# The layout of the transposed embedding rows: feature by feature instead of sample by sample

## The reference

```python
e = jnp.stack([tbl_0[ids[:, 0]], ..., tbl_26[ids[:, 26]]], axis=1)     # (512, 27, 128)
dot_products = jnp.einsum('bnd,bmd->bnm', e, e)                          # the "gram", one 27 x 27 per sample
r, c = np.tril_indices(27, k=-1)
z = dot_products[:, c, r]
h = jnp.concatenate([z, dense_ctx], axis=1)
h = jnp.maximum(h @ W_top1 + b_top1, 0.0)
h = jnp.maximum(h @ W_top2 + b_top2, 0.0)
y = h @ W_top3
```

## Time and profile before

| | |
|---|---|
| three runs | 153.29, 154.19, 155.78 us |
| the profiled execution | 153.77 us, span 152.0 us |
| PE busy, matmuls / weight loads | 106.0 us / 91.7 us |
| DVE busy | 65.1 us |
| ACT busy | 69.8 us |
| POOL busy | 69.1 us |
| mean granted clock of TensorE | 0.84 |

### The profile page before, as it was taken

One profiled execution on the slowest core, in us unless ns is written; L12 is line 12 of the kernel. 1 busy time (PEld: TensorE's weight loads), 2 busy tenths in 40 slices (PEclk: granted clock), 3 DMA queues, 4 the chain that ended last, 5 costly groups with the idle time before them and its releaser, 6 DMA issues.

```text
span 152.0 us, 3526 instructions
## 1 busy us (share of the span) xinstructions
PE 106.0 (70%) x1530; PEld 91.7 (60%) x1530; DVE 65.1 (43%) x96; ACT 69.8 (46%) x116; POOL 69.1 (45%) x74
## 2 busy tenths in 40 slices
PE   5987999993994190101143279999949949996694
PEld 5854778872893180000022169998849749896592
DVE  6699999997546300000063003898103212200500
ACT  3369999999280350000070007693406404660342
POOL 4778788787777777777057705407000000000000
PEclk9999999999689558555555556999999996999999
DMA  3976776796635551211002100201000000000000
GB/s 87 245 182 178 201 229 182 182 299 192 189 109 165 138 138 52 54 52 52 17 17 52 52 22 17 56 0 35 17 9 0 4 4 4 0 4 4 0 4 1
DMA packets 5433, 12.33 MB, mean 81 GB/s; under 512 B 1829, under 2 KB 2341, under 8 KB 5418
## 3 DMA queue, kind: packets, MB, share of 16 engines
q1 hardware_dynamic: 3306, 7.78, 18.3%
q0 software_dynamic: 2112, 4.33, 11.1%
HBM read 12.10 MB, written 0.00 MB: 80 GB/s over the span
## 4 chain that ended last, share of the span: by engine, by line
PE 41%; issue 31%; ACT 15%; DVE 7%; DMA 3%; SPq 2%; ACTq 0%
PE gram_ps L460 10%; PE ring L433 10%; PE ring L489 9%; ACT away L612 5%; PE ring L504 5%; DVE marks L553 4%; PE ring L444 4%; DMA raw<-tbl 3%; ACT high L598 3%; ACT marks L624 2%; DVE low L538 2%; ACT rowsT L657 2%; ACT rowsT L647 1%; PE ring L514 1%; SPq L322 1%
## 5 line engine op out<-in xcount | busy, mean ns | idle before, releaser
L360 POOL DMA_INDIRECT rows<-tbl,ids_sb x66 | 68.2, 1034 | 36.1 <-issue 18.9
L553 DVE TENSOR_TENSOR marks<-ids_ps,row_no 125x768 fp32r<-125x768 f32 (+1 forms) x38 | 39.7, 1077 | 36.6 <-remote 29.8
L460 PE MATMUL gram_ps<-rowsT 128*27 128x27 f32 x1024 | 16.1, 201 | 31.2 <-issue 31.2
L433 PE MATMUL ring<-marks,high 125*128 125x384 f32 (+1 forms) x92 | 36.5, 396 | 0.8 <-DVE low L538 0.5
L433 PE MATMUL ring<-marks,low 125*128 125x384 f32 (+1 forms) x92 | 35.3, 384 | 0.0
L460 PEld LDWEIGHTS gram_ps<-rowsT 128*27 128x27 f32 x1024 | 13.1, 112 | 34.6 <-issue 34.4
L433 PEld LDWEIGHTS ring<-marks,high 125*128 125x128 f32 x92 | 19.0, 206 | 4.2 <-DVE low L538 1.4
L433 PEld LDWEIGHTS ring<-marks,low 125*128 125x128 f32 x92 | 19.0, 206 | 1.4
L657 ACT COPY rowsT<-ring 128x512 f32<-128x512 f32 (+2 forms) x15 | 8.1, 555 | 21.5 <-remote 20.5
L647 ACT COPY rowsT<-ring 128x384 f32<-128x384 f32 (+1 forms) x11 | 11.1, 1009 | 14.0 <-remote 6.6
L538 DVE TENSOR_TENSOR low<-raw,high 125x512 fp32r<-125x512 f32 (+1 forms) x24 | 16.9, 705 | 0.0
(11 more groups left out here) (39 smaller groups left out, 76.2 us busy)
## 6 DMA issues: line engine op xcount, KB each, us to landing
raw<-tbl SPq DMA_DIRECT2D x9, 448.0 KB
raw<-tbl SPq DMA_DIRECT2D x2, 560.0 KB
rows<-tbl,ids_sb POOLq DMA_INDIRECT x66
w_sb<-w SPq DMA_DIRECT2D x2, 256.0 KB
w_sb<-w SPq DMA_DIRECT2D x1, 512.0 KB
raw<-tbl SPq DMA_DIRECT2D x9, 52.0 KB
raw<-tbl SPq DMA_DIRECT2D x2, 224.0 KB
w_sb<-w SPq DMA_DIRECT2D x1, 192.0 KB
```

The costliest lines, as they stand in the source:

```text
L360: nc.gpsimd.indirect_dma_start(out=rows[0:n, i % ROW_BUFS, s, :], out_offset=None, in_=tables[PLACES[s]], in_offset=bass.IndirectOffsetOnA ...
L433: last = nc.tensor.matmul(bank[:, 0:n], part[:, i % SPLIT_BUFS, c * D:(c + 1) * D], mark_of(unit, c), start=c == 0 and part is high, stop= ...
L460: last = nc.tensor.matmul(gram_ps[s * STRIP:s * STRIP + F, g, 0:F], places, places, start=True, stop=True)
L553: nc.vector.tensor_tensor(marks_of(unit), index.to_broadcast([TP, c1 - c0, n]), which.to_broadcast([TP, c1 - c0, n]), ALU.is_equal).then_i ...
```

## The change

`rowsT` becomes `[P, F, B]`: 27 features, and for each of them the 512 samples side by side. The padding goes. The features of one sample are now 512 floats, 2048 bytes, apart. The copy behind a find job writes one unbroken run of 512 or 384 floats. The copy behind a turn writes up to four runs of 128 floats and reads PSUM in its own order. The gram's two operands are the same 27 floats on each partition as before, read at a step of 2048 bytes, where they were side by side. Nothing else changes: no step, wait, engine, or count of instructions, and each engine keeps its order.

```diff
-F_PITCH = -(-F // PER_BANK) * PER_BANK
...
-        rowsT = sb("rowsT", [P, B, F_PITCH])
-        rowsT_f = rowsT[:, :, :].rearrange("p b f -> p f b")
+        rowsT = sb("rowsT", [P, F, B])
...
-                            places = rowsT[:, b0 + s * STRIP + g, 0:F]
+                            places = rowsT[:, 0:F, b0 + s * STRIP + g]
                             last = nc.tensor.matmul(gram_ps[s * STRIP:s * STRIP + F, g, 0:F], places, places,
                                                     start=True, stop=True)
...
-                    nc.scalar.copy(rowsT_f[:, place_of(i), b0:b0 + n],
+                    nc.scalar.copy(rowsT[:, place_of(i), b0:b0 + n],
                                    ring_bank(step)[:, 0:n]).then_inc(taken, 1)
...
-                    nc.scalar.copy(rowsT[:, b0:b0 + n, group[0]:group[-1] + 1],
-                                   src.rearrange("p (f b) -> p b f", b=n)).then_inc(taken, 1)
+                    nc.scalar.copy(rowsT[:, group[0]:group[-1] + 1, b0:b0 + n],
+                                   src.rearrange("p (f b) -> p f b", b=n)).then_inc(taken, 1)
```

## The result

The changed kernel took 158.8 us in the median of four runs (157.99 to 160.86); the kernel before, with one run more, 154.64 us. The ratio is 1.028, with a 95% interval of 1.017 to 1.039. In a later set of runs it was 1.046 (1.034 to 1.057). So it is slower in both sets, though the first interval doesn't settle whether by more than 2%; 158.8 us lies near the forecast of 157.5 and inside its range of 152.5 to 171. Some runs of each set were disturbed and took longer: the medians hold them, the ratios leave them out, so a ratio need not be the quotient of two medians, and for pad2052, held_before and held_again too few undisturbed runs were left to give one. The profiled execution took 158.86 us, its span is 157.0 us, 5.0 more than before.

A forecast was written before the change was run, and what follows sets the result against it. DVE and ACT are full from 8 to 38 us, gram 0 stalls from 47 to 77, PE is full outside the grams from 91; 153.77 + 3.5 + 0.2 - 0 = 157.5 us, range 152.5 to 171.

The forecast's parts named there:

- I took 0 with 1.1 as the end: ACT's shorter find copies, 5.8 us in all: 0 gained on the path, -1.1 us as the other end.
- no loss: Turn copies on ACT: neither gain nor loss, already 0.84 ns a float and now reading PSUM in order.
- +1.17 us: Bursts of each of grams 1 to 3: 3.69 us where 2.52, together 3.5 us.
- ACT's 1.97 ns a float: ACT's cost of single floats 112 bytes apart, taken for PE's gram columns: 28.8 ns a matmul.
- the pauses I keep as they are: Pauses inside grams 1 to 3: unchanged, though a slower burst could hide a few tenths of each.
- all of it reaches the end: Grams 1 to 3 have a full PE behind them, so their whole 3.5 us lengthens the kernel.
- I gave its burst 0.2 us: Gram 0's last 87 matmuls at half clock add 2.5 ns each, 0.2 us.
- Reads that hide it: Rival for the grams: PE fetches ahead, bursts stay at 2.5 us, 153.8 or 152.7 us; chance 0.24.
- A strip in series: Rival for the grams: a strip's loads and passes don't overlap, 53 ns a matmul, 169 us; chance 0.10.
- A shared path at 106 ns a matmul: Rival for the grams: four strips share one read path, 13.6 us a gram, 194 us; chance 0.08.
- the crawl: Gram 0's single records with idle time from 57 us; a shorter crawl had chance 0.10, a longer one 0.08.
- Loads and passes: In the grams, loads run beside passes and four strips beside each other: 24.3 ns estimated at half clock, 26.3 seen.

The follow-up runs named there:

- pad2052: The changed kernel with one float of padding behind each feature (step of 2052 bytes), second chip: 119.27 us against 119.35 for the kernel before, no ratio.
- held_before: The kernel before, with POOL's gathers of tile 2 held until gram 0 is done, second chip: 119.09 us against 119.35, no ratio.
- held_again: The kernel before, with POOL's gathers of tile 2 held until gram 0 is done, first chip: 149.26 us against 153.53, no ratio.
- copies_only: The changed kernel with both gram operands 27 floats side by side (what is computed is changed): 153.41 us against 153.51 for the kernel before, ratio 0.9964.
- pad2064: The changed kernel with four floats of padding behind each feature (step of 2064 bytes): 153.1 us against 153.51 for the kernel before, ratio 0.9953.
- step112: The kernel before, its gram reading one feature of 27 samples 112 bytes apart (what is computed is changed): 153.4 us, ratio 1.0033.
- second pair: The kernel before and the changed kernel, traced once more on the first chip: the span grows by 3.1 us, from 152.2 to 155.3.
- after_again: The changed kernel once more, against the kernel before on the first chip: 159.51 us, ratio 1.046 (1.034 to 1.057).

## Why the prediction was right

The forecast's direction and nearly its size were right, but much of that is luck: the mechanism that it priced costs this kernel nothing, and one that it hadn't foreseen, the collision of two 2048-byte steps, made it slower.

**Copies.** Right in size (0.58 and 0.49 us for the find copies) and in place: DVE and the empty stretch cover them, and copies_only shows a gain of less than 1.2 us where I took 0 with 1.1 as the end. What I had wrong is "no loss" for turn copies: they don't get longer by their own pattern (0.59 us), but the one beside gram 1 does, to 3.83 us. It ends inside the gram, and from gram 1 to gram 2 it takes 6.43 us where it took 6.41, so it cost nothing.

**Gram time.** The direction was right and two sizes were off, in opposite ways. I had +1.17 us for the bursts of each warm gram: 3.69 us forecast, 6.4 measured, +3.9. The step that failed is the one that took PE's cost from ACT's 1.97 ns a float at 112 bytes and ran loads and passes beside each other, both of them estimates; for steps other than 2048 it is a fair estimate (28.8 ns forecast, 32 measured in pad2064 and step112), and for 2048 on both operands it is not. The other step was "the pauses I keep as they are". They went: 1.99, 1.98 and 1.35 us. Net a gram costs +1.9, +1.9 and +2.5 us, where I had 1.17.

Pad2064 is the case that my working describes: far floats, with bursts of 4.0 to 4.14 us, somewhat longer than my 3.69. By my sum, in which all of that reaches the end, it would be over 4 us slower. It is not slower at all (ratio 0.9953), since shorter pauses and the clock behind gram 2 give the time back. So the step "all of it reaches the end" failed too, and without the collision of two 2048-byte steps the forecast of a slower kernel would have been wrong.

**Gram 0.** I gave its burst 0.2 us because at half clock, by my estimate, the array wants a column only every 1.80 ns. Its burst grew by 2.1 us and its end came 2.4 us later (0.9 in the second pair of traces), since a matmul takes 51 ns there, at half clock, as it takes 50 at full clock.

**Given back.** The 86 records between grams 2 and 3 take 10.0 us at full clock where they took 11.7 at 0.85, and a pause of 1.06 us after gram 3 is gone. I had no term for this. In the kernel before, the windows behind gram 2 and the layer's records there read:

```profile
124.70:128.20 3.50, 3.50 (x17) 3.50 (x18) 1.58 (x4) 1.37 (x4) 0.00 (x0) 0.51 0.02 5
128.20:136.40 8.20, 8.20 (x71) 7.53 (x69) 0.78 (x3) 5.03 (x12) 0.00 (x0) 1.00 0.00 0
...
124.58 4.57 PE L489 MATMUL ring<-zT,w_sb 128*128 128x128 f32 x24
```

The clock is at half for 3.5 us, just behind the pause of 1.98 us in gram 2; in the changed kernel, without the pause, it stays at 1.00, and the same 24 records take 3.02 us. The same holds in the second pair (4.58 and 3.00 us). That there is a pause doesn't decide it alone, since pad2064 has one of 1.53 us there and its clock stays at 1.00 as well. The sum of my terms, 3.7 us, is near the 5.0 measured because larger errors cancel: +10 us in the bursts (gram 0's among them), -5.3 in the pauses, -3.9 in the clock and the stretches between.

**Rivals.** Reads that hide it: PE doesn't hide them, since every pair of far operands takes 32 ns or more; but the rival's outcome, no slower kernel, is what every far step tried except 2048 on both operands gave. A strip in series: its 53 ns is near the 50 measured, but its mechanism isn't what the runs show, since pad2064 has the same reads in the same order at 32, and its 169 us is 10 us too long. A shared path at 106 ns a matmul falls. That the change would hardly move the crawl was right: gram 0's last burst begins at 88.99 us where it began at 88.66.

**Loads and passes.** That they run beside each other was my estimate, from the 26.3 ns of a matmul at half clock. The traces agree as far as one can see for dense reads and for far ones off 2048 bytes: dense, a matmul takes 19.7 ns where loads and passes in turn would take 4 x 27 x 0.90 / 4 = 24.3 (an estimate, from the 0.90 ns a column in the prediction), and both operands 112, 2052 or 2064 bytes apart (32 ns) cost no more than one at 2048 (34 and 35). With both at 2048 bytes a matmul takes 50 ns, and there the estimate doesn't hold. Why a far float costs PE more than a dense one, no run shows.

**Open.** Why 2048 bytes collide (pad2064 shows that it is the step; other large powers of two weren't tried), what makes the clock fall behind a dense gram 2 and not behind a slower one, what stalls the first chip, and how large the loss is: 2.8 and 4.6% in the two sets. The changed kernel itself wasn't run on the second chip. There gathers run beside grams 1 and 2, and may slow the dense ones too, so its cost there can't be read from these runs.

## What to carry to other kernels

When both operands of an f32 matmul are read float by float at a fixed step, don't let both steps be 2048 bytes: a padding of four floats here gives back what the layout cost (ratio 0.9953, a gram of 4.14 us for 6.41), and one float brings the gram down as far (4.16 us, on the second chip). A burst that got longer beside a pause for which the profile names nobody wasn't charged in full here (pad2064's three grams: 4.6 us more in the bursts, 1.4 to 1.9 in all); cost the pair, and look at the clock behind it (4.57 or 3.00 us for the same 24 records). Where a stall of 30 us has no cause that the trace shows, run the kernel on a second chip before building a version around it. And when a forecast comes out right, run the case that it described: here pad2064 showed that the case costs nothing.

## What the runs showed of the hardware

- Far floats on both operands make a gram's bursts about 1.6 us longer (32 against 19.7 ns a matmul), the same at 112, 2052 and 2064 bytes. ACT's find copies that write floats 112 bytes apart take 1147 ns for 512 floats and 895 for 384, with unbroken runs 576 and 490.
- Both operands at a 2048-byte step: 51 ns a matmul at half clock and 50 at full (4.40 us for 172 records, 6.41 for 256), where one operand at 2048 has 34 or 35. Other engines beside it were slowed: ACT's copy 3.83 for 0.59 us (3.98 in after_again), two of DVE's 2.32 for 0.48 us (2.87).
- PE's pauses of 0.3 to 2.5 us in bursts of small matmuls ended 1.2 to 1.6 us after a 16 KB packet of the instruction queue, 47 of 47 times.
- POOL's gathers beside a dense gram: 3.64 for 2.12 us on the same chip, in one execution of each kernel.
- Two chips, one program: 153.5 and 119.4 us. The difference is a stall of 20 to 35 us, which goes along with long runs of gathers on one chip and isn't there on the other.
